# Second attention layer: the next batch's key scores, diagonal and transposes moved ahead in each solve stretch, with two buffers for GpSimd's input

## The reference

```python
s = jnp.einsum('bihd,bjhd->bhij', k, k) * scale      # keys against keys
s = jnp.where(strict, s, -jnp.inf)                   # only j < i
...
p = e / jnp.where(denom == 0, 1.0, denom)            # softmax of s over j
L = p * beta.transpose(0, 2, 1)[..., None]
A = L + jnp.eye(T)
u = solve_triangular(A, v, lower=True)
sc = jnp.einsum('bihd,bjhd->bhij', q, k) * scale     # ordinary causal attention
attn = softmax(where(causal, sc, -inf))
o = jnp.einsum('bhij,bhjd->bihd', attn, u) ... @ Wo
```

## Time and profile before

| what | us |
|---|---|
| span of the profiled execution (first to last instruction) | 830.0 |
| median of the 3 timed runs | 836.22 |
| lowest of them | 832.2 |
| highest of them | 967.87 |
| PE busy with matmuls in the span | 509.5 |
| DVE busy | 553.3 |
| ACT busy | 299.9 |
| POOL busy | 226.2 |

### The profile page before, as it was taken

How to read it: one execution, slowest core, us unless ns; L and a number is a source line. 1 busy time by engine, 2 the same in 40 slices (tenths; PEclk the granted TensorE clock), 3 DMA queues, 4 the chain that set the end, 5 groups by cost and what they waited for, 6 DMA issues and landing times. The chain is left out here.

```text
span 830.0 us, 17909 instructions
## 1 busy us (share of the span) xinstructions
PE 509.5 (61%) x7444; PEld 422.6 (51%) x7444; DVE 553.3 (67%) x1066; ACT 299.9 (36%) x716; POOL 226.2 (27%) x320
## 2 busy tenths in 40 slices
PE   0363557865958533455556565757777660899980
PEld 0253446754747423334444453545555450899980
DVE  6999699897689847757617772556664155667834
ACT  3363423642556220064440522443313150365520
POOL 3000000000000001007817818803850026043344
PEclk9775666977889776755588576868979655899996
DMA  8435050050000103740250032200101062656214
GB/s 310 160 65 105 1 115 1 2 114 1 2 1 1 51 0 70 152 88 4 54 102 7 8 71 53 48 6 7 11 9 12 11 276 81 255 192 224 95 54 136
DMA packets 52066, 61.29 MB, mean 74 GB/s; under 512 B 25408, under 2 KB 45392, under 8 KB 47504
## 3 DMA queue, kind: packets, MB, share of 16 engines
q1 hardware_dynamic: 50176, 55.15, 24.9%
q0 software_dynamic: 1808, 4.99, 2.0%
HBM read 45.24 MB, written 13.63 MB: 71 GB/s over the span
## 5 line engine op out<-in xcount | busy, mean ns | idle before, releaser
L881 PE MATMUL psum<-arena 32*32 32x16 f32 (+16 forms) x5608 | 354.0, 273 | 232.3 <-DVE arena L1550 74.5
L881 PEld LDWEIGHTS psum<-arena 128*32 128x32 f32 (+7 forms) x5608 | 282.7, 128 | 302.6 <-DVE arena L1550 76.8
L1987 POOL TENSOR_TENSOR arena<-arena 128x31 f32<-128x31 f32 (+15 forms) x124 | 68.0, 548 | 9.7
L1985 POOL TENSOR_TENSOR arena<-arena 128x31 f32<-128x31 f32 (+15 forms) x124 | 64.4, 519 | 9.7
L1343 ACT ACTIVATE psum<-psum,arena 128x256 f32<-128x256 f32 (+7 forms) x128 | 45.7, 370 | 26.8 <-DVE arena L1611 26.6
L1312 ACT ACTIVATE arena<-psum 128x512 f32<-128x512 f32 (+1 forms) x48 | 35.3, 736 | 48.3 <-PE psum L881 48.2
L1621 DVE TENSOR_REDUCE arena<-psum 128x2 f32<-128x512 f32 (+1 forms) x48 | 41.3, 860 | 13.6 <-PE psum L881 12.9
L1520 DVE TENSOR_TENSOR_SCAN arena<-arena 128x255 f32<-128x255 f32 x64 | 42.5, 726 | 11.4 <-ACT arena L1255 11.3
L1965 POOL DMA_DIRECT2D arena<-wq x1 | 0.9, 862 | 171.9 <-PE psum L881 171.9
L1998 POOL TENSOR_TENSOR fc_second_parts<-arena,fc_first_parts 128x2048 fp32r<-128x2048 f32 x6 | 27.9, 4648 | 63.8 <-ACT fc_first_parts L1431 63.8
L1255 ACT ACTIVATE arena<-arena 128x255 f32<-128x255 f32 x64 | 27.2, 498 | 46.6 <-DVE arena L1506 46.6
(11 more groups left out here) (179 smaller groups left out, 955.6 us busy)
## 6 DMA issues: line engine op xcount, KB each, us to landing
arena<-fc SPq DMA_DIRECT2D x16, 1024.0 KB, 5.2
arena<-parts SPq DMA_DIRECT2D x40, 256.0 KB, 4.6
parts<-arena SPq DMA_DIRECT2D x16, 384.0 KB, 3.5
arena<-parts SPq DMA_DIRECT2D x40, 128.0 KB, 5.5
dispatched<-arena SPq DMA_DIRECT2D x1, 2048.0 KB, 18.5
arena<-arena SPq DMA_DIRECT2D x128, 8.0 KB, 1.8
arena<-dispatched SPq DMA_DIRECT2D x8, 256.0 KB, 3.0
expert_rows<-arena SPq DMA_DIRECT2D x8, 256.0 KB, 2.3
```

The source lines that it names most:

```text
L881: return nc.tensor.matmul(out, lhsT, rhs, start=start, stop=stop)
L1985: link(G_.tensor_tensor(tmp, A3[:, k + 1:BLK, k:k + 1].to_broadcast([P, rows, w]), X3[:, k:k + 1, 0:w].to_broadcast([P, rows, w]), ALU.mult))
L1987: ins = G_.tensor_tensor(X3[:, k + 1:BLK, 0:w], X3[:, k + 1:BLK, 0:w], tmp, ALU.add)
```

## The change

`kdiag`, `den` and `blocks` of batch 1 move ahead of `probs` 0 in the part before stretch 0. In stretches 0 and 1 `kscores` and `kmax` of the batch after next come first, and behind them, as soon as its turn comes, one group `kdiag`, `den`, `blocks` of that batch; the head of each stretch no longer holds `den` and `blocks`. In stretch 0 gate, `proj`, `split`, `vproj` of batch 3 stand in the middle and the scores of batch 1 last; in stretch 1 the output of batch 0 stands in the middle. `lag` lets go of all held steps before a `den`. `blkA` and `cT` get two buffers each; the small arrays `ncc`, `beta` and `cT` move into the unused half of the `masks` table. `blocks` b waits for the inverse of batch b - 2 in place of b - 1. GpSimd's wait for `invT_ready` stays, and so do `blkX` and `diag` with one buffer.

```diff
@@ -256,7 +256,7 @@
     o += groups("kscores", 1, 0) + [("kmax", 1, 0)] + groups("scores", 1, 0)[:4] + [("kdiag", 0), ("den", 0), ("blocks", 0)]
     o += groups("kprobs", 1, 0) + groups("scores", 1, 0)[4:] + [("minus", 1, 0), ("max", 1, 0)]
     o += groups("kscores", 1, 1) + [("kmax", 1, 1)] + keys_then_queries(2)
-    o += groups("probs", 1, 0) + [("qload", 2), ("kdiag", 1)] + groups("kprobs", 1, 1) + [("vproj", 2)]
+    o += [("kdiag", 1), ("den", 1), ("blocks", 1)] + groups("kprobs", 1, 1) + groups("probs", 1, 0) + [("qload", 2), ("vproj", 2)]
 
     def one_each(steps):
         return [[step] for step in steps]
@@ -268,15 +268,18 @@
         return [[("oT", 1, b)], [("wo", 1, b), ("gate", 3, b)]]
 
     p1, p2, p3 = (one_each(groups("probs", 1, b)) for b in range(1, B))
-    ahead = [queries(1) + one_each(groups("kscores", 1, 2)) + [[("kmax", 1, 2)], [("gate", 2, 3)], [("proj", 1, 3, 1), ("split", 1, 3, 1)],
-                                                             [("proj", 1, 3, 0), ("split", 1, 3, 0)], [("vproj", 3)], [("kdiag", 2)]],
-             [[("otr", 1, 0)]] + p1[:3] + [[("oT", 1, 0)]] + p1[3:6] + out(0)[1:] + p1[6:] + [[("qload", 3)]]
-             + one_each(groups("kscores", 1, 3)) + [[("kmax", 1, 3)]] + queries(2)[:4] + [[("kdiag", 3)]] + queries(2)[4:],
+    def inverted(b):
+        return one_each(groups("kscores", 1, b)) + [[("kmax", 1, b)]], [[("kdiag", b), ("den", b), ("blocks", b)]]
+
+    (k2, d2), (k3, d3) = inverted(2), inverted(3)
+    ahead = [k2 + [[("gate", 2, 3)], [("proj", 1, 3, 1), ("split", 1, 3, 1)]] + d2 + [[("proj", 1, 3, 0), ("split", 1, 3, 0)], [("vproj", 3)]]
+             + queries(1),
+             k3 + [[("otr", 1, 0)]] + d3 + p1[:3] + [[("oT", 1, 0)]] + p1[3:6] + out(0)[1:] + p1[6:] + [[("qload", 3)]] + queries(2),
              [[("otr", 1, 1)]] + p2[:3] + [[("oT", 1, 1)]] + p2[3:6] + out(1)[1:] + p2[6:] + queries(3),
              [[("otr", 1, 2)]] + p3[:3] + [[("oT", 1, 2)]] + p3[3:6] + out(2)[1:] + p3[6:]]
     for b in range(B):
 
-        solve = [[("inverse", b)] + ([("den", b + 1), ("blocks", b + 1)] if b + 1 < B else []) + [("solve", b, 0, 0), ("solve", b, 0, 1)]]
+        solve = [[("inverse", b), ("solve", b, 0, 0), ("solve", b, 0, 1)]]
         for s in range(1, NS):
             solve += [[(kind, b, s - (kind == "update"), half) for half in range(2)] for kind in ("update", "solve")]
         o += sum(spread(solve, ahead[b]), [])
@@ -308,6 +311,9 @@
 
     o, held, solving = [], [], False
     for step in order:
+        if step[0] == "den":
+            o += held
+            held = []
         chain = step[0] in ("inverse", "update", "solve", "den", "blocks")
         if step[0] == "inverse":
             solving = True
@@ -488,13 +494,14 @@
                  for _ in range(2)]
         ublk = take(NS * Q4 * BLK).rearrange("p (s q e) -> p s q e", s=NS, q=Q4)
         diag = take(BLK * BLK)
-        blkA = take(BLK * BLK)
+        blkAs = [take(BLK * BLK) for _ in range(2)]
         blkX = take(BLK * BLK)
         blkT = take(BLK * BLK // 4)
         invT = [take(BLK * BLK) for _ in range(2)]
-        cT = take(BLK)
-        beta = [take(NS * Q4) for _ in range(2)]
-        ncc = [take(NS * Q4) for _ in range(B)]
+        spare = c_["masks"][:, 2 * P:4 * P]
+        ncc = [spare[:, b * NS * Q4:(b + 1) * NS * Q4] for b in range(B)]
+        beta = [spare[:, P + i * NS * Q4:P + (i + 1) * NS * Q4] for i in range(2)]
+        cTs = [spare[:, P + 2 * NS * Q4 + i * BLK:P + 2 * NS * Q4 + (i + 1) * BLK] for i in range(2)]
         nbias = take(NS * Q4)
         stack["k", 2] = take(H * T // 2).bitcast(BF16).rearrange("p (h t) -> p h t", h=H)
         vz.append(take(NS * Q4 * HD).rearrange("p (s q e) -> p s q e", s=NS, q=Q4))
@@ -1746,11 +1753,11 @@
                 elif kind == "blocks":
 
                     b = step[1]
-                    if b:
-                        dve.wait_ge(inv_ready, b)
+                    if b >= 2:
+                        dve.wait_ge(inv_ready, b - 1)
                     wait_done(dve, ("kdiag", b), "act")
-                    st(V.transpose(cT, ncc[b]))
-                    st(V.transpose(blkA.rearrange("p (i j) -> p i j", i=BLK), diag.rearrange("p (n i) -> p i n", i=BLK)))
+                    st(V.transpose(cTs[b % 2], ncc[b]))
+                    st(V.transpose(blkAs[b % 2].rearrange("p (i j) -> p i j", i=BLK), diag.rearrange("p (n i) -> p i n", i=BLK)))
                     settle()
                     V.nop().then_inc(blocks_ready, 1)
                 elif kind == "inverse":
@@ -1973,9 +1980,9 @@
                     pool.wait_ge(blocks_ready, b + 1)
                     if b:
                         pool.wait_ge(invT_ready, b)
-                    A3 = blkA.rearrange("p (i j) -> p i j", i=BLK)
+                    A3 = blkAs[b % 2].rearrange("p (i j) -> p i j", i=BLK)
                     X3 = blkX.rearrange("p (i j) -> p i j", i=BLK)
-                    link(G_.tensor_tensor(A3, A3, cT.unsqueeze(2).to_broadcast([P, BLK, BLK]), ALU.mult))
+                    link(G_.tensor_tensor(A3, A3, cTs[b % 2].unsqueeze(2).to_broadcast([P, BLK, BLK]), ALU.mult))
                     link(G_.memset(blkX, 0.0))
                     link(G_.affine_select(out=X3, in_=X3, compare_op=ALU.not_equal, fill=1.0, base=0,
                                           pattern=[[1, BLK], [-1, BLK]], channel_multiplier=0))
```

## The result

The changed kernel takes 821.19 us (median of 4 runs, 820.28 to 821.44) against 834.3 us for the kernel before: ratio 0.9859, 95% interval 0.9829 to 0.989, so 1.1 to 1.7% faster. One of the four runs of the kernel before, at 967.87 us, is far slower than the rest and stays out of the ratio (without it the median before is 832.4 us). The forecast was 829.1 us, 0.9% less, taken as no change that a measurement can tell. Most of this study goes to the part of the gain that was not forecast.

The account below looks back on a forecast made before the run. No engine was full in stretches 0 and 1; a chain of short PE and DVE steps bound the kernel. Terms summed to -5.1 us, span 830.0 to 824.9; plus 4.2 gave 829.1 us, range 817 to 838.

Parts of the forecast that it names:

- Turn 0 to 1: From `inverse` 1 to first copy of `solve` 1.0: moving batch 3's `split` earlier cuts 17.13 to 8.14 us, -9.0.
- Before stretch 0: `kdiag` 1 fills PE's idle hole before `probs` 0's second group, and a wait for ACT goes: -1.3 us.
- `den`, `blocks` out of the heads: Their 2.9 us on DVE leave the stretch heads, with no gain: 0, bounds -1.1 and 0.
- `den`, `blocks` 2 in the middle: Mid-stretch 0: they lengthen a run of DVE work without gaps, +2.9 us, bounds 0 and +2.9.
- updates' -2.0: Stretches 0 and 1: smaller updates on PE stand beside the busy steps, -2.0 us, bounds 0 and -3.9.
- `kdiag` 3: Stretch 1: PE waits 3.6 us for the moves of the maxima, 0.7 more behind DVE: +4.3 us.
- rival A: Waits in the middle (`kdiag` 3, `blocks` 2) fall into holes and cost nothing: 821.9 us, chance 0.22.
- Two buffers: End of stretch 2: second GpSimd input buffer starts the fourth inverse 3.1 us earlier, but `pv` 2 limits it: -1.0 us.
- GpSimd beside DVE: DVE's scalings slow down while GpSimd inverts beside them: +1.0 us, bounds 0 and +4.3.
- rival B: The hole is only moved: GpSimd's sharing takes its upper bound or `kdiag` 2 also waits: 832.4 us, chance 0.16.
- C: Rival: slower, as `kscores` groups waiting for ACT's slots hold the solve chain on PE: 843.9 us, chance 0.12.
- The signs: Profile marks named beforehand, among them stretch 0 with its turn 7 to 9 us less, stretch 1 2 to 4 longer.

Follow-up runs that it names:

- experiment 1: Kernel before, with SP alone taking both `split` steps of batch 3 behind the moves of `solve` 0.7: 824.35 us, before 833.0.
- Experiments 3 and 5: 3: kernel before, `kdiag` 1 and `kprobs` 1 ahead of `probs` 0, 823.9 us; 5: kernel before, SP's batch 2 loads behind `solve` 0.0, 826.05 us.
- experiment 8: Changed kernel with `den` and `blocks` of batches 2 and 3 back in the heads of stretches 1 and 2: 822.24 us.
- experiment 9: Changed kernel with `kdiag`, `den`, `blocks` 3 three `probs` groups later in stretch 1: 817.11 us.
- experiment 2: Kernel before with gate, `proj`, `split`, `vproj` of batch 3 behind the fourth scores group, key scores and `kdiag` 2 still late: 837.88 us, before 833.0.
- experiment 4: Kernel before with `qload` 2 listed behind `vproj` 2, which left SP's order the same: 832.65 us, before 833.0.

## Why the prediction was right and wrong

- **Turn 0 to 1, -9.0: right.** Measured -7.9, and with SP's order alone -9.1 (experiment 1). The cause, eight stack loads ahead of four small moves in SP's order, is shown. The missing 1.1 us is the clock in 160 matmuls (6.89 us for 5.84); the turn 1 to 2, for which nothing was forecast, grew by 1.0 us in the same way (6.80 us at 0.59). All five profiles of the changed kernel and its variants show the latter (9.0 to 9.2 us at a clock of 0.56 to 0.58, and 7.9 to 8.5 at 0.61 to 0.66 in the others), so the lower clock goes with the new order there, and the forecast had no term for it.
- **Before stretch 0, -1.3, bounds 0 and -4.3: this step failed.** Measured -7.3. What the step did weigh came: 0.9 us of the hole behind `proj` and 0.4 of the small waits make its 1.3. But it read PE's rows only up to 420.73. The next two idle times of the same timeline, 2.08 and 3.36 us with releaser "issue", belonged to the very steps that the change moves (`kprobs` 1 and `vproj` 2), and they had neither a term nor a bound. These 5.4 us are gone; the last 0.5 is PE's clock. Experiments 3 and 5 show in their place that the order and the loads of batch 2 decide over these waits.
- **How the miss adds up.** This step missed by 6.0 us and the span by 5.8 (824.9 predicted, 819.1 measured), but that the two agree is luck: the misses elsewhere cancel. Stretch 1 came out 3.6 us under its forecast and the rest 1.6; the turn 0 to 1, the turn 1 to 2 and the piece ahead of the first rotation came out 1.1, 1.0 and 2.4 us over theirs. The other 2.1 of the 7.9 us in the timed runs are the 4.2 us that the forecast put on top of the span: the four runs of the changed kernel lie 1.8 to 1.9 us above theirs.
- **`den`, `blocks` out of the heads, 0, bounds -1.1 and 0: too small for the first head.** From `inverse` 0 to the first copy it was 4.92 us and is 2.41, so 2.5 us go. Behind that copy stretch 0 grew by 4.2 us (56.74 to 60.91). The forecast of +1.4 us for stretch 0, measured +1.7, is in part luck.
- **`den`, `blocks` 2 in the middle, +2.9: fits, but isn't shown.** DVE has no gap around L1759, as was foreseen, and is busy 2.9 us less in stretch 0 without them (experiment 8). But the stretch also holds two new "issue" waits, 3.96 us in sum, for which the forecast had no term, and a lower clock (0.66 for 0.72). So neither this price nor the updates' -2.0 can be read from it.
- **`kdiag` 3, +4.3: right place, price too high.** The wait was forecast at 3.6 us and is 3.15; but at most 1.5 us of it was on the path (experiment 9), and stretch 1 is no longer than the same stretch in three other profiles with the order of before. The rest fell into time that the chain waited for anyway, the first part of rival A's thought.
- **Two buffers, -1.0: mechanism right.** GpSimd starts right behind L1769, DVE's 4.02 us of waiting are gone, stretch 2 is 3.9 us shorter at the same clock of 0.87, and `pv` 2, which now ends last, gives 3.5 back at the turn: -0.4 in sum.
- **GpSimd beside DVE, +1.0: did not come.** The 28 scalings from `inverse` 1 to `inverse` 2 took 7.20 us before and take 6.44 after (L1780 there), the next 28 7.62 and 7.39. Stretch 0's grew by 0.2. In sum DVE spends 0.8 us less on them, so the upper bound of +4.3 is far off. No run shows what that bound, and rival B's figure with it, puts into the sum, each scaling held for a whole GpSimd instruction of 0.55 us: in these two windows of the changed kernel one takes 0.23 and 0.26 us on the mean.
- **The rivals.** The time came out at A's figure (821.9) and not for A's reason: of the prices of the middle at least a part was paid, and the lead paid for it. B did not happen in the change, but does in experiment 2. C did not happen: PE's wait for ACT's slots in the two stretches is 14.2 us against 14.8.
- **The signs.** The DMA wait before `pv` 0, `kdiag` 3's wait, GpSimd's start and PE's wait at turn 2 to 3 came as named, DVE's wait before the first copy of `solve` 1.0 nearly so (7.27 us). Two didn't: stretch 0 with its turn fell by 6.2 us and not by 7 to 9, and stretch 1 grew by 1.2 and not by 2 to 4.
- **What counts as no change.** The forecast put 2% as what a measurement can tell, and gave 0.91 to a change within it, which is where the 1.4% lie. But the interval reaches only 0.3% to either side, so a change far under 2% was there to be told, and the forecast's own -5.1 us, 0.6%, need not have counted as none.

## What to carry to other kernels

A small transfer that the next step waits for should stand ahead of bulk loads in its queue; here moving the bulk in the issuing engine's program alone took the turn from 17.13 to 8.03 us (experiment 1), with no change of the compute order. Read all idle times of an engine in every piece that a reorder touches, those released by "issue" too: where they stand between two instructions of one kind, look at the DMA view's instruction queue. When the consumer of a small move is placed right behind its producer, the hole comes back there (6.18 us of waiting in experiment 2, 3.15 us before `kdiag` 3 in the changed kernel). Before an experiment is read, ask which engine's list the edit changes; the edit of experiment 4 changed none. And before 1 or 2 us of one piece are given to a cause, look at the same piece in other profiles and at the clock beside it.

## What was not expected of the hardware

PE seems to wait for its own instructions. In the kernel before it stood still for 2.08 and 3.36 us while 2.75 MB of stack loads were in flight between 411 and 432 us; with the loads issued later, in the same order of matmuls, 0.63 us was left. The instruction packet that began at 419.7 without the loads began at 422.7 beside them, and all 30 such waits between 400 and 530 us in the 13 profiles end 1.2 to 1.8 us after a packet has landed. Loads are not the only cause. In stretch 0 of the changed kernel PE waits 2.20 us at 464.29, before the first stack load there is issued (468.82). Its four variants wait at the same matmuls, for 1.90 to 2.31 us, and the kernel before doesn't. The packet that ends the wait took 1.39 us, with nothing else moving; why it began only at 461.3 was not tried. The second wait there, 1.76 us at 476.89, falls beside the loads.
